# Token-order x3 from accumulating transpositions, and a new order of the router stage

## The reference

```
x1 = x  + tanh(g) * attention(layernorm(x), ctx)
x2 = x1 + tanh(g) * ternary_ffn(layernorm(x1))
# third layer: selective scan over ctx; the gate z is layernorm(x2) read as (batch, channel, time)
y  = (scan + D * u) * silu(z);  x3 = x2 + tanh(g) * swapaxes(y, 1, 2)
# fourth layer: 64 experts, 8 for each token, 128 places for each expert
logits = layernorm(x3) @ router;  probs = softmax(logits);  top 8, weights over their sum
out = x3 + tanh(g) * sum of the chosen experts' results, in order of arrival, those over 128 dropped
```

## Time and profile before

| | us |
|---|---|
| median of 3 runs (lowest, highest) | 423.9 (423.41, 425.51) |
| span of the profiled execution | 422.3 |
| PE busy | 353.7 (84%) |
| DVE busy | 312.5 (74%) |
| ACT busy | 263.5 (62%) |
| POOL busy | 282.6 (67%) |
| mean granted TensorE clock | 0.923 |

### The profile page before, as it was taken

The page is one execution under the profiler, slowest core; times in us unless marked ns, Lnnn a source line. Parts: engine busy times, 40 slices in busy tenths (PEclk is TensorE's granted clock), DMA queues, the critical chain, the costliest instruction groups (busy, mean ns, idle before and its releaser), DMA issues.

```text
span 422.3 us, 7244 instructions
## 1 busy us (share of the span) xinstructions
PE 353.7 (84%) x2035; PEld 257.3 (61%) x2035; DVE 312.5 (74%) x696; ACT 263.5 (62%) x530; POOL 282.6 (67%) x228
## 2 busy tenths in 40 slices
PE   4936954798989899989987179999999999999990
PEld 2422642354454345645687067899888888899880
DVE  3999899899997989899987946645554545453556
ACT  0999999999887598797272435444544444544420
POOL 4200045799997999999623477787787778778840
PEclk9986885699999699999999559999999999999996
DMA  8920603569989789889101247989889888875558
GB/s 238 371 100 0 164 0 130 177 222 308 284 288 308 254 286 315 258 302 288 68 2 50 76 113 190 210 212 223 219 213 218 220 209 206 219 149 103 86 87 262
DMA packets 63482, 80.52 MB, mean 191 GB/s; under 512 B 7058, under 2 KB 43714, under 8 KB 63458
## 3 DMA queue, kind: packets, MB, share of 16 engines
q1 hardware_dynamic: 53456, 64.43, 49.2%
q0 software_dynamic: 8832, 15.74, 18.6%
q10 hardware_dynamic: 1170, 0.08, 0.2%
HBM read 70.13 MB, written 10.09 MB: 190 GB/s over the span
## 4 chain that ended last, share of the span: by engine, by line
PE 41%; POOL 15%; DVE 10%; DMA 8%; issue 6%; ACT 2%; SPq 0%; DVEq 0%; POOLq 0%
PE bank L1300 10%; PE bank L1338 8%; POOL ssm L590 7%; PE bank L1293 5%; DMA ssm<-routed,idx 5%; PE bank L1148 4%; PE bank L1094 3%; PE bank L1280 3%; POOL sums L676 2%; PE bank L1121 2%; DVE bank L1537 2%; DVE ssm L1542 2%; POOL ffn L609 2%; POOL ssm L595 2%; DMA du<-sums 1%
## 5 line engine op out<-in xcount | busy, mean ns | idle before, releaser
L1542 DVE TENSOR_TENSOR_SCAN ssm<-ssm,bank 128x512 f32<-128x512 f32 x64 | 78.1, 1221 | 4.6 <-issue 2.5
L665 POOL DMA_INDIRECT ssm<-routed,idx x64 | 66.4, 1037 | 21.8 <-issue 13.7
L590 POOL TENSOR_TENSOR ssm<-ssm,bc_buf 128x1024 f32<-128x1024 f32 x31 | 73.0, 2355 | 10.1 <-DVE ssm L1542 3.4
L676 POOL DMA_INDIRECT sums<-ssm,idx x40 | 67.2, 1681 | 14.5 <-issue 9.7
L1767 DVE SCALAR_TENSOR_TENSOR ssm<-ssm,bank 128x96 f32<-128x96 f32 x64 | 20.0, 313 | 75.0 <-ACT ssm L964 74.9
L1300 PE MATMUL bank<-ssm,wguT 128*128 128x256 bf16 x576 | 72.4, 272 | 0.0
L1300 PEld LDWEIGHTS bank<-ssm,wguT 128*128 128x128 bf16 x576 | 56.1, 98 | 11.9 <-DVE ssm L1759 0.3
L964 ACT ACTIVATE ssm<-bank 128x96 f32<-128x96 f32 x64 | 16.1, 251 | 74.4 <-PE bank L1338 74.4
L1094 PE MATMUL bank<-ssm,ident 128*128 128x512 f32 x98 | 48.9, 613 | 8.5 <-POOL ssm L590 6.0
L1338 PE MATMUL bank<-arena,ssm 128*128 (+1 forms) x256 | 54.0, 334 | 1.6 <-ACT ssm L947 1.0
L1148 PE MATMUL bank<-xs,wguT 128*128 128x512 bf16 x192 | 48.6, 407 | 4.6 <-POOL xs L574 4.2
(11 more groups left out here) (227 smaller groups left out, 693.6 us busy)
## 6 DMA issues: line engine op xcount, KB each, us to landing
bc_buf<-bc_rows SPq DMA_DIRECT2D x32, 512.0 KB, 4.4
ssm<-bc_rows SPq DMA_DIRECT2D x22, 512.0 KB, 5.4
arena<-in_L_ffn_gate_proj SPq DMA_DIRECT2D x32, 192.0 KB
arena<-in_L_ffn_up_proj SPq DMA_DIRECT2D x32, 192.0 KB
arena<-in_L_ffn_down_proj SPq DMA_DIRECT2D x32, 192.0 KB
B_last<-bc_rows SPq DMA_DIRECT2D x10, 512.0 KB, 5.4
sums<-zero_f SPq DMA_DIRECT2D x1, 2304.0 KB, 14.1
arena<-in_L_ffn_w_gate_up SPq DMA_DIRECT2D x1, 2048.0 KB, 11.5
```

Of the source, the lines that this page charges most:

```text
L590: pool.tensor_tensor(prod[:, a:b, :], hs[:, a:b, :], C_buf[:, a:b, :], ALU.mult).then_inc(s.prod_ok, 1)
L665: pool.indirect_dma_start(out=xe[:, k, :], out_offset=None, in_=routed, in_offset=bass.IndirectOffsetOnAxis(ap=idx2[:, k, 0:1], axis=0)).t ...
L676: pool.indirect_dma_start(out=sums, out_offset=bass.IndirectOffsetOnAxis(ap=idx2[:, k, 1:2], axis=0), in_=ye[:, k, :], in_offset=None, com ...
L1542: dve.tensor_tensor_scan(hs[:, k % 4, :], dA[:, k % 3, :], x[:, :], 0.0, ALU.mult, ALU.add).then_inc(s.scan_ok, 1)
```

## The change

`own_part` and `add_y` become transpositions (`is_transpose=True`) that accumulate in PSUM: x3 of tile j starts as x2T turned back, and y2 is added turned. `own_part` so reads x2T and waits for its copies. On TensorE the second half's logits move ahead of the second half of x3, and both `positions` go behind it. ScalarE makes the even tiles of `gate_z` first, and `gated(c, h)` waits only for the tiles of its half. VectorE moves `gated(0, 1)` ahead of `mean_over_deviation(3, 1)`, and `select(1)` ahead of `shifts(0)`.

```diff
@@ gate_z(c), ScalarE
-                for j in range(4 * c, 4 * c + 4):
+                for j in (4 * c, 4 * c + 2, 4 * c + 1, 4 * c + 3):
@@ own_part(c), TensorE
+                pe.wait_ge(s.xn4T_sb, 2 * c + 2)
                 for j in range(4 * c, 4 * c + 4):
                     if j == 6:
                         pe.wait_ge(s.y_sb, 4)
-                    pe.matmul(x3_of(j), ident[:, :], x_res[:, j, :], start=j % 2 == 0, stop=False, skip_group_check=True)
+                    for kc in range(2):
+                        pe.matmul(x3_of(j)[:, kc * P:kc * P + P], x2T[:, kc, j * P:j * P + P], ident[:, :], start=j % 2 == 0 and kc == 0, stop=False,
+                                  is_transpose=True, skip_group_check=True)
@@ add_y(c)
-                        ins = pe.matmul(x3_of(j)[:, h * P:h * P + P], u[:, h, j * P:j * P + P], ident[:, :], start=False, stop=h == 1, skip_group_check=True)
+                        ins = pe.matmul(x3_of(j)[:, h * P:h * P + P], u[:, h, j * P:j * P + P], ident[:, :], start=False, stop=h == 1, is_transpose=True, skip_group_check=True)
@@ order on TensorE
-            turn_x2(0)
-            own_part(0)
-            turn_x2(1)
-            logits_of_x2(0)
...
+            turn_x2(0)
+            logits_of_x2(0)
+            turn_x2(1)
+            own_part(0)
             logits_of_y(0)
             add_y(0)
+            logits_of_x2(1)
+            logits_of_y(1)
             own_part(1)
-            logits_of_x2(1)
+            add_y(1)
             pe.wait_ge(s.c_ident, 4)
             positions(0)
-            logits_of_y(1)
-            add_y(1)
             positions(1)
@@ gated(c, h), VectorE
-                dve.wait_ge(s.z_sb, 4 * c + 4)
+                dve.wait_ge(s.z_sb, 4 * c + 2 * h + 2)
@@ order on VectorE
             gated(0, 0)
+            gated(0, 1)
             mean_over_deviation(3, 1)
-            gated(0, 1)
...
             half_statistics(4, 0, x3_of, s.x3_ps)
+            select(1)
             shifts(0)
-            select(1)
```

## The result

| | before | changed |
|---|---|---|
| median of the runs at the first comparison (lowest, highest), us | 423.79 (423.41, 425.51) | 419.38 (418.04, 420.59) |
| ratio, 95% interval | | 0.9897 (0.9865 to 0.9929) |
| span of the profiled execution, us | 422.3 | 416.3 |
| mean granted TensorE clock | 0.923 | 0.929 |

Medians are of all executions; the ratios, and the means and counts of executions further down, leave out those over 1.5% above the fastest of the same kernel. The stage that the prediction worked out behaves as it said. These are instructions of the changed kernel in order of time, to be held against the earlier trace rows; the first of them, the first piece of x2 on VectorE, is the zero from which I count.

What follows compares the result with a forecast made beforehand. The chain of waits between scan and experts, mostly TensorE ahead of VectorE's second selection, was taken as the bound. VectorE's 2.75 us gain less 0.5 lost on GpSimd gave 2.2: 423.9 to 421.7 us, range 420.4 to 424.0.

Steps and rivals of the forecast that it cites:

- A transposition's price: TensorE's own_part and add_y: eight accumulating transpositions take 0.87 us, saving 0.86 and 0.97 per half.
- The first half hidden: TensorE's first-half moves, ahead of the logits of y2, cost nothing: the wait for gated(0, 1), until 217.3, covers them.
- The gating moves: gate_z and gated: logits of y2 start 0.24 us earlier, the first selection 0.14 earlier.
- VectorE is late next: VectorE bounds the second selection, starting about 224.0, 0.3 us behind its logits; second statistics 2.75 us earlier.
- GpSimd takes 0.5 back: GpSimd's second rstd waits for weights(0), losing 0.5 us of VectorE's gain; the second shift comes 2.2 us earlier.
- The sum: Whole kernel: 2.2 us off both, span 422.3 to 420.1 and median 423.9 to 421.7; chance 0.48.
- Rival 2: First experts: the clock rises early against the work, 0.5 to 1 us more won, 420.9; chance 0.15.
- rival 1: First experts: 2.2 us more run at half clock, giving back 1.1 of the gain, 422.8; chance 0.20.
- that 1.6: Whole kernel: the 423.9 us median lies 1.6 above the profiled span of 422.3, taken as unchanged.
- Rival 4: Router stage of the changed kernel: TensorE's clock falls and stays low through the logits, slower at about 426.6; chance 0.10.

Runs made afterwards that it cites:

- rstd_first: Changed kernel with GpSimd's second rstd ahead of weights(0) and VectorE's top_sum(0) behind shifts(1); median 418.60 us, ratio 0.9857 to the kernel before.
- look_4: Changed kernel, no edit, profiled once more; first gather 30.79 us behind the start of x2, first place-product 20.40 us after that; no median given.
- look_2: Kernel before, no edit, profiled once more; first gather 35.96 us behind the start of x2, first place-product 19.19 us after that; no median given.
- warm: Changed kernel with 44 filler products of zeros on TensorE ahead of the first experts; median 419.41 us, ratio 0.9865 to the kernel before.
- again: Changed kernel, no edit, measured once more; median 419.16 us, ratio 0.9872 to the kernel before.
- transposes: Kernel before with own_part and add_y as accumulating transpositions alone, every order as before; median 421.48 us, ratio 0.9957.
- pe_order: Kernel before with the new TensorE order and select(1) ahead of shifts(0), plain products and old gating kept; median 420.74 us, ratio 0.9936.
- gates: Kernel before with the gating part alone: even gate_z tiles first, gated waiting for its half, gated(0, 1) moved ahead; median 422.78 us, ratio 0.9987.
- before_fill: Kernel before with six products of zeros in TensorE's pause ahead of logits_of_y(0); median 422.59 us, ratio 0.9970.
- shift_first: Changed kernel with shifts(0) ahead of select(1) on VectorE again; median 421.15 us, ratio 0.9926 to the kernel before.
- plain: Changed kernel with own_part and add_y as plain products again; median 420.20 us, ratio 0.9914 to the kernel before.
- look_1: Kernel before, no edit, profiled once more; first gather 32.71 us behind the start of x2; no median given.
- control: Kernel before, no edit, measured against itself; median 423.27 us, ratio 0.9983.

## Why the prediction was wrong, point by point

- **A transposition's price.** Right: an accumulating one costs what the other does, 0.88 for eight.
- **The first half hidden.** Right: `logits_of_x2(0)` waits 1.04 for x2, the copies wait for nobody, and the logits of y2 start 0.7 us behind the end of `own_part(0)`.
- **The gating moves.** Right: first selection 11.70 behind x2, 11.92 before; 0.22 and not 0.14. Alone they bring 0.3.
- **VectorE is late next.** Right: selection at 15.49 where 15.6 was said, behind logits that were 0.3 earlier.
- **GpSimd takes 0.5 back.** Right in the trace: the second statistics are 2.9 earlier (17.78 behind x2, 20.72 before), the shift 2.45. Undoing it brought the gather nothing, as rstd_first showed.
- **The sum.** 2.2 in the text for the router stage, 2.4 measured, in every profile in which the clock held there.
- **Rivals 1 and 2, the first experts.** Rival 2 and not the likelier rival 1: in the first pair of profiles 0.7 us is won, where the clock came back 1.5 us earlier against the work and one scatter no longer waits. It is partly luck of the execution, since look_4 lacks it and look_2 has it with the kernel before. warm shows no more to be had.
- **The step that failed** is "I take that 1.6 as lying around the span and unchanged, so a saving is subtracted from either". I took the 423.9 as the time of an execution like the profiled one with 1.6 us around it. It is a mixture. Of before's 89 executions, 55 have a mean clock below 0.929; they take 424.8 us on average, the other 34 take 422.1. Of the changed kernel's 12 (the first comparison and again), 2 are below, and the other 10 take 419.0. Between executions that are not below, the gain is 3.1, what the first pair of profiles says behind the start of x2. The rest, 1.3 of the 4.4 between the means of all (423.8 and 419.4), is that low-clock executions are rarer, a term that the sum did not have. With the 0.2 that the sum was short and the 0.7 of rival 2, the 2.2 become 4.4; without the 1.3 the median would lie inside the range. The border at 0.929 was chosen after seeing the clocks, and as transposes shows, a low mean clock is not the same event in every kernel; pe_order, where the same working gives 1.3 for stages that gain 1.2, is the check on it.
- **Rival 4, the clock in the router stage,** named the right mechanism and the wrong kernel. I read 1.00 in one profile of before and took it as a property of the kernel. The fall happens in before (look_2, 3.3 us, from the start of the logits of y2 on), and filling that pause takes 1.6 us off before's mean while the marks of the stage stay (18.54 and 32.70). In the changed kernel the pause is 0.7 us and not 1.46, and the plain product of `logits_of_x2(0)` stands between the transpositions. The counts of executions below 0.929 go with this pause: 55 of 89 at 1.46 us (before), 6 of 11 at 1.14 (gates), 2 of 12 at 0.70 (changed), 1 of 12 at about 0.15 in both pe_order and before_fill. It is not the pause alone: shift_first, with the changed kernel's order on TensorE, has 4 of 11, plain, with no pause there, 2 of 11, and rstd_first 1 of 6. Of seven profiles with the old order, fillers in that pause left aside, two show the fall there (look_2, transposes), of nine with the new one look_4, at 0.5 us.

The rule of the Trainium skill that I weighed ("TensorE: Matmul & The Clock Gate", section "Part 4: PE-mode transpose": transpositions do not count as activity for the clock the way products do) fits transposes, where the clock fell behind 24 transpositions, a plain product and a pause, and look_4, where it fell at the start of 16 of them. But look_2 fell with plain products in the place of 8 of them, and the changed kernel's other three profiles held. The prediction also misread the trace of before where it said that no stretch of transpositions alone is longer than 0.87 us. That is so in the router stage; earlier, 16 of them (L1051) take 1.89:

```profile
41.05 1.97 PE L1051 MATMUL bank<-ident,wguT 128*128 128x128 f32 x16
42.94 3.73 PE L1057 MATMUL bank<-wpT,dtT 8*128 8x512 f32 x8
```

```profile
42.00:43.00 1.00, 1.00 (x11) 0.83 (x9) 1.00 (x1) 1.00 (x2) 0.00 (x0) 1.00 0.08 16
46.00:47.00 1.00, 1.00 (x3) 0.40 (x2) 1.00 (x1) 1.00 (x4) 0.00 (x0) 0.74 0.36 125
```

The clock held through them and fell only between 46 and 47, with plain products on TensorE since 42.94. No run here isolates the rule.

What stays open: how much of the 1.3 us is the router stage's fall alone. before_fill says up to 1.6, at the edge of its interval; the counts of profiles are small, and a low mean clock can come from the scan stage or the last experts as well. look_1 shows that: mean clock 0.927, no fall in the router stage, one among the last experts.

## What to carry to other kernels

A single profile is one execution. Before a saving is subtracted from a median, look at the mean clock of all executions: where it spreads, the median can hold an event that the profile does not show. A pause on TensorE ahead of a dense stretch can cost more than its length (3.3 us behind one of 1.45 in look_2), and an order that puts hidden work there can be worth more than the chain of waits says. And once a chain's engine is relieved, look at what the next engine shares with its neighbours before undoing the next wait.

## What was unexpected of the hardware

- The clock's fall in the router stage is a matter of the execution: same program, 1.00 throughout in before, control and look_1, 0.50 from 216 to 222.9 in look_2.
- The start of x2, with no changed line ahead of it, lies between 204.95 and 208.97 us over these profiles, and at 211.67 in before_fill's.
- The time from the first gather to the first place-product has two values, 19.2 to 19.8 and 20.4 to 20.5 us, and goes with the moment at which the clock comes back (up to 8.8 us behind the gather, or 9.5 and more).
- A VectorE instruction of 4 elements a row took 0.68 us beside GpSimd's multiplication in rstd_first, and 0.16 in the changed kernel without it.
- Products of zeros hold the clock: 1.00 from 231 to 245 us in warm, where the changed kernel has 0.50 until 244.7. They did not keep it from falling at 227 first.
